# GNN layer with BatchNorm and LayerNorm on one core: other places for the gathered edge groups, bf16 parts read in place, and a row phase in eight pieces

## What is computed

```
msg   = x[src] + edge_feat                       # 53125 x 128
neigh = segment_sum(msg, dst, 3125)
rst   = (1 + eps) * x + neigh
h     = rst @ W1 + b1                            # 3125 x 256
h     = relu((h - mean(h,0)) * rsqrt(var(h,0) + 1e-5) * gamma + beta)
out   = layernorm(x + h @ W2 + b2)               # rows of 128
```

## Time and profile before

| | us |
|---|---|
| median of 3 runs | 280.74 (280.03 to 281.6) |
| the profiled execution | 281.48 |
| its span, first to last instruction | 279.7 |
| PE busy | 244.9 |
| weight loads | 200.6 |
| VectorE busy | 208.4 |
| ScalarE busy | 131.7 |
| GpSimd busy | 181.2 |

### The profile page before, as it was taken

The page is one execution under the profiler, slowest core; times in us unless marked ns, Lnnn a source line. Parts: engine busy times, 40 slices in busy tenths (PEclk is TensorE's granted clock), DMA queues, the critical chain, the costliest instruction groups (busy, mean ns, idle before and its releaser), DMA issues.

```text
span 279.7 us, 7102 instructions
## 1 busy us (share of the span) xinstructions
PE 244.9 (88%) x2211; PEld 200.6 (72%) x2211; DVE 208.4 (75%) x916; ACT 131.7 (47%) x236; POOL 181.2 (65%) x117
## 2 busy tenths in 40 slices
PE   1567989999998889988899999999999859999970
PEld 1456768899987677766788888777878648844870
DVE  3888997788998778778489887876867861178990
ACT  0327864455555535545255544444443302086494
POOL 2078888888888888888888888888888920000000
PEclk9999999999999999999599999999999968999995
DMA  5955766687888777788488888776665200000033
GB/s 165 285 172 108 147 145 137 156 191 197 189 195 185 178 164 171 181 179 183 96 172 192 174 195 171 167 179 145 150 126 105 53 2 0 2 0 1 2 114 116
DMA packets 49535, 38.39 MB, mean 137 GB/s; under 512 B 5083, under 2 KB 48523, under 8 KB 49497
## 3 DMA queue, kind: packets, MB, share of 16 engines
q1 hardware_dynamic: 32829, 30.62, 38.2%
q0 software_dynamic: 14976, 6.82, 20.4%
q10 hardware_dynamic: 1692, 0.48, 0.9%
HBM read 36.31 MB, written 1.60 MB: 136 GB/s over the span
## 4 chain that ended last, share of the span: by engine, by line
PE 46%; DMA 16%; issue 14%; POOL 9%; DVE 7%; ACT 4%; SPq 2%; DVEq 0%; ACTq 0%; POOLq 0%
PE ps L641 18%; PE ps L649 12%; DMA egat<-in_x_dram,srci 9%; POOL egat L402 9%; DMA egat<-in_edge_attr_dram 7%; PE ps L679 5%; PE ps L673 4%; PE ps L595 4%; ACT big L527 3%; PE ps L665 2%; SPq L321 1%; DVE big L1033 1%; DVE big L1035 1%; PE ps L670 1%; DVE hit_l L904 1%
## 5 line engine op out<-in xcount | busy, mean ns | idle before, releaser
L402 POOL DMA_INDIRECT egat<-in_x_dram,srci x104 | 172.2, 1656 | 44.0 <-issue 29.2
L488 ACT ACTIVATE big<-ps 128x500 f32 x156 | 95.1, 610 | 119.8 <-PE ps L679 91.6
L641 PE MATMUL ps<-big,xp 128*128 128x114 f16 (+8 forms) x675 | 116.9, 280 | 0.2 <-issue 0.2
L649 PEld LDWEIGHTS ps<-hit_c,ebuf 128*128 128x128 f32 x624 | 101.8, 194 | 16.6 <-DVE aggT L983 6.1
L649 PE MATMUL ps<-hit_c,ebuf 128*128 128x20 f32 x624 | 95.1, 230 | 9.1 <-DVE aggT L983 5.0
L641 PEld LDWEIGHTS ps<-big,xp 128*128 128x128 bf16 x675 | 63.0, 110 | 14.6 <-issue 1.1
L983 DVE TENSOR_TENSOR aggT<-aggT,ps 128x20 f32 x208 | 35.8, 172 | 49.8 <-PE ps L649 39.7
L910 DVE TENSOR_TENSOR hit_k<-iota_k,key 128x400 f16<-128x400 f16 x156 | 56.1, 359 | 0.0
L904 DVE TENSOR_TENSOR hit_l<-iota_k,lo 128x256 f16<-128x256 f16 x156 | 52.1, 334 | 1.7 <-issue 1.6
L679 PE MATMUL ps<-hit_k,hit_l 128*128 128x400 f16 x156 | 52.3, 335 | 0.0
L908 DVE TENSOR_TENSOR hit_k<-iota_k,key 128x300 f16<-128x300 f16 x156 | 48.2, 309 | 0.0
(11 more groups left out here) (101 smaller groups left out, 165.5 us busy)
## 6 DMA issues: line engine op xcount, KB each, us to landing
ebuf<-in_edge_attr_dram SPq DMA_DIRECT2D x78, 256.0 KB
egat<-in_edge_attr_dram SPq DMA_DIRECT2D x51, 128.0 KB
egat<-in_x_dram,srci POOLq DMA_INDIRECT x104
out_dram<-big SPq DMA_DIRECT2D x6, 256.0 KB
w_sb<-in_L_gnn_W_dram ACTq DMA_DIRECT2D x2, 128.0 KB, 6.8
rows<-in_dst_dram SPq DMA_DIRECT2D x1, 192.0 KB
rows<-in_src_dram ACTq DMA_DIRECT2D x1, 192.0 KB
egat<-in_edge_attr_dram SPq DMA_DIRECT2D x1, 66.0 KB
```

The lines of the kernel that those rows point to most:

```text
L402: return nc.gpsimd.indirect_dma_start(to, None, x[:, :], bass.IndirectOffsetOnAxis(ap=ix, axis=0), compute_op=op)
L488: nc.scalar.activation(cnt[:, :, bass.ds(lows[m % LOADS], WIN)], ps[:, m % BANKS_C, 0:KEYS].rearrange("p (t n) -> p t n", n=WIN), ACT.Copy ...
L641: last = nc.tensor.matmul(ps[:, ACC + f % 2, 0:SIZES[f]], xp[:, t, n, :], cnt[:, t, STARTS[f]:STARTS[f] + SIZES[f]], start=(u == 0), stop= ...
L649: last = nc.tensor.matmul(ps[:, SUMS + w % BANKS_S, 0:WIN], rows_v[:, j * D:(j + 1) * D], hits_v, start=(j == 0), stop=(j == ROWS - 1))
```

## The change

1. **Places of the gathered windows.** `arrange` replaces `in_window`. It walks through the windows with a running cost `now` in PE cycles and takes the next gathered group as soon as now has reached GATHER_FIRST + n * GATHER. 207 stays the last gathered window.
2. **bf16 parts in place.** `xp` and ScalarE's 14 copies go. The matmuls read the upper halves of xN and of a full-size `xr` where they lie, every second 16-bit value; only the third part has a tile of its own (`x3`).
3. **GpSimd's addition of b2** now waits for the last block's product (`block_multiplied`, 9), since xN is read until then.
4. **Ring of `hit_k`, `hit_l`:** 8 places instead of 6.
5. **Row phase:** eight pieces of 4, 4, 4, 4, 4, 2, 2 and 1 row tiles on eight banks. ReLU of half 1 of blocks 5 and 6 goes to ScalarE (one step instead of two). Piece 6 is normalised by VectorE from PSUM. VectorE takes the statistics of a piece ahead of the shifts of the piece before.

```diff
-RING_K = 6
+RING_K = 8
+ROUNDS = 12
+SUM = 670
+COUNT = 770
+KEPT = 810
+HITS = 2400
+TURN = 1680
+GAP = 14
+GATHER = 9360
+GATHER_FIRST = 27000
+ACT_FROM = 5
...
-    def in_window(w):
-        return (w + 1) * NG // G > w * NG // G
+    def arrange():
+        order = [(w + 1) * NG // G > w * NG // G for w in range(G)]
+        for _ in range(ROUNDS):
+            ready = spans([w for w in range(G) if not order[w]])
+            now, m, n, order = 0, 0, 0, []
+            for w in range(G):
+                gathered = n < NG - 1 and w < G - 1 and (m == GC or now >= GATHER_FIRST + n * GATHER)
+                gathered = gathered or w == G - 1
+                f, u0, u1 = share(ready, w)
+                own = SUM if gathered else max(SUM + COUNT + KEPT * (m < KEEP), HITS)
+                now += own + (u1 - u0) * (SIZES[f] + GAP) + TURN * (X_RATE * w < NT)
+                order.append(gathered)
+                m, n = m + (not gathered), n + gathered
...
+    ROW_PIECES = [(t, t + 4) for t in range(0, NT - 5, 4)] + [(NT - 5, NT - 3), (NT - 3, NT - 1), (NT - 1, NT)]
...
         xN = sb("xN", [P, NT, D])
-        xp = sb("xp", [P, NT, PARTS, D], BF16)
+        xr = sb("xr", [P, NT, D])
+        x3_room = sb("x3_room", [P, NT * D // 2])
+        x3 = x3_room[:, :].bitcast(BF16).rearrange("p (t d) -> p t d", d=D)
...
                 pool.wait_ge(x_rest_made, NB)
-                pool.wait_ge(x_first_made, NB)
+                pool.wait_ge(block_multiplied, F)
...
+                if b >= ACT_FROM:
+                    hb = hT[:, 1, b * BANK:b * BANK + width(b)]
+                    nc.scalar.activation(hb, hb, ACT.Relu, scale=scl[:, 1:2], bias=sft[:, 1:2]).then_inc(relu_half0_made, 1)
...
+            deviation(0)
+            for a in range(1, 5):
+                deviation(a)
+                normalise(a - 1)
+            normalise(4)
+            deviation(5)
+            deviation(6)
+            normalise(5)
+            deviation(7)
+            normalise(7)
...
-                        last = nc.tensor.matmul(ps[:, ACC + f % 2, 0:SIZES[f]], xp[:, t, n, :],
+                        part_v = x3[:, t, :] if n == 2 else upper((xN, xr)[n][:, t:t + 1, :])[:, 0, :]
+                        last = nc.tensor.matmul(ps[:, ACC + f % 2, 0:SIZES[f]], part_v,
...
-            for b in range(NB):
+            for b in range(ACT_FROM):
                 r = rl[:, b % 2, 0:width(b)]
...
+            for a in range(len(ROW_PIECES)):
+                stats(a)
+                if a > 0:
+                    shifts(a - 1)
+                moments(a)
+            t0, t1 = ROW_PIECES[6]
+            dve.wait_ge(row_shifts_made, 7)
+            for t in range(t0, t1):
+                k = (t - t0) * D
+                nc.vector.tensor_scalar(oN[:, t, :], ps[:, 2, k:k + D], lrs[:, t:t + 1], lnb[:, t:t + 1],
+                                        ALU.mult, ALU.add).then_inc(late_rows_normalised, 1)
+            shifts(7)
```

More of the change, by code:

```diff
@@ L82, in gnn_layer, with spans, share @@
     KEYS = NT * WIN
-    def in_window(w):
-        return (w + 1) * NG // G > w * NG // G
-    C_AT = [w for w in range(G) if not in_window(w)]
-    G_AT = [w for w in range(G) if in_window(w)]
+    UNITS = NT * PARTS
+    def spans(c_at):
+        return [c_at[g - 1] + SETTLE for g in ENDS[:-1]] + [G]
+    def share(ready, w):
+        for f in range(F - 1):
+            if ready[f] <= w < ready[f + 1]:
+                n, i = ready[f + 1] - ready[f], w - ready[f]
+                return f, UNITS * i // n, UNITS * (i + 1) // n
+        return 0, 0, 0
+    def arrange():
[11 more added lines that the diff above has]
+                m, n = m + (not gathered), n + gathered
+            short = NG - sum(order)
+            at = [w for w in range(G) if not order[w]]
+            for w in at[len(at) - short:] if short > 0 else []:
+                order[w] = True
+        return order
+    IN_WINDOW = arrange()
+    C_AT = [w for w in range(G) if not IN_WINDOW[w]]
+    G_AT = [w for w in range(G) if IN_WINDOW[w]]
     C_OF = {w: m for m, w in enumerate(C_AT)}
     G_OF = {w: n for n, w in enumerate(G_AT)}
-    READY = [C_AT[g - 1] + SETTLE for g in ENDS[:-1]] + [G]
-    UNITS = NT * PARTS
+    READY = spans(C_AT)
     def units(w):
[L95 to L99, removed]
+        return share(READY, w)
+    ROW_PIECES = [(t, t + 4) for t in range(0, NT - 5, 4)] + [(NT - 5, NT - 3), (NT - 3, NT - 1), (NT - 1, NT)]
     EARLY = STARTS[-1] // BANK
@@ L1035, in _ @@
                 nc.vector.tensor_scalar(hb, r, 0.0, None, ALU.max).then_inc(relu_half1_made, 1)
[L1037 to L1054, removed]
-                                                   in1=lrs[0:r, t0:t1], op0=ALU.mult,
-                                                   op1=ALU.mult).then_inc(row_shifts_made, 1)
@@ new lines, in stats, with moments @@
+            def stats(a):
+                t0, t1 = ROW_PIECES[a]
+                r = rows_of(t1 - 1)
+                dve.wait_ge(rows_made, a + 1)
+                for t in range(t0, t1):
+                    k = (t - t0) * D
+                    nc.vector.bn_stats(lst[0:r, t, :], ps[0:r, (a + 4) % 8, k:k + D]).then_inc(row_stats_made, 1)
+            def moments(a):
+                t0, t1 = ROW_PIECES[a]
+                r = rows_of(t1 - 1)
+                for t in range(t0, t1):
+                    dve.wait_ge(row_stats_made, t + 1)
+                    nc.vector.bn_aggr(lag[0:r, t, :], lst[0:r, t, :]).then_inc(row_moments_made, 1)
```

92 lines of the change are left out of this document (42 added, 50 removed).

## The result

The changed kernel takes 292.09 us (median of 4 runs, 291.27 to 292.7), beside 280.38 us (279.57 to 281.6) for the kernel before on the same chip: a ratio of 1.041, 95% interval 1.036 to 1.046, so 11.7 us slower. Its profiled execution took 291.68 us, its span is 289.9.

A forecast was written before the change was run, and what follows sets the result against it. GpSimd's gather stream, one group per 3.8 us, was taken to bound PE where it waits. Loop +12.0, addition 0, parts 0, tail +0.3 made +12.3 on 281.48: 293.8 profiled, 293 us as median, range 285 to 300.

The forecast's parts named there:

- window 184 starts: PE, window of group 50: gathered rows there at 216.0 us, plus 1.1 for the clock, so start at 217.1 us.
- work behind it, to the hidden layer: PE's windows from 184 on and last block's products, at full clock without the stall: 38.2 us.
- end of the loop against before: Loop over the windows: ends at 255.3 us against 243.27, +12.0 us.
- addition of b2 beside the hidden layer: GpSimd's addition after the loop: covered or not held up, bounds 0 and 7.6 us, taken as 0.
- parts in place, copies, ring of eight: Front copies and ring gain 0; spread weight loads cost 0 to 10 us, taken as 0.
- row phase: Tail after the hidden layer: earlier statistics against more hand-overs, bounds -1.0 and +1.3 us, taken as +0.3.
- The stream: GpSimd's gathers: 33 groups after group 17 at 3.81 us each, rows on PE 2.7 us after the last gather ends.
- The term of 1.1 us: PE's lateness from half clock shortly before window 184, taken between 0 and 2.4 us.
- This sign of the forecast: PE's waits for gathered rows in the new profile: far above 7.9 us, some 20 to 25 us in 35 or more.
- The rival that it holds VectorE up after the loop: GpSimd's addition of b2 delays the last block's addition and hidden layer by 7.6 us: 300.6 us, chance 0.05.
- The rival of slow loads: PE's spread weight loads are slow, adding up to 10 us: some 298 to 303 us, chance 0.08.
- two readings of the Trainium skill: PE's weight loads: strided columns load fast, cost stays 0; or 32-bit reads leave half the bits unused, cost rises.

The follow-up runs named there:

- half_the_gathers: The changed kernel, same places, with GpSimd gathering only one of the two rows per partition, so the sums are incomplete: 261.68 us (one run).
- new_places_only: The kernel before with only the new places of the gathered windows: 300.47 us, ratio 1.075.
- places_by_pe_cost: The changed kernel with planner constants HITS 1440 instead of 2400, GATHER 9120 and GATHER_FIRST 20000: 264.90 us, ratio 0.946.

## Why the prediction was right

It held, in sign, in size (293 against 292.09) and in its mechanism: window 184 had to wait for group 50's rows, and 39 us of counted work stood behind it. That the two numbers lie 0.9 us apart is partly luck. Of the steps below one is 2.3 us too late, one 0.8 us too short and one 0.6 us too long, and they partly cancel; and between the profiled executions the loss is 291.68 - 281.48 = 10.2 us where +12.3 was forecast, while the medians lie 11.7 us apart. Step by step:

| step | predicted | measured |
|---|---|---|
| window 184 starts | 217.1 us | 214.8 |
| work behind it, to the hidden layer | 38.2 us | 39.0 |
| end of the loop against before | +12.0 us | +10.5 |
| addition of b2 beside the hidden layer | 0 | 0 |
| parts in place, copies, ring of eight | 0 | 0 |
| row phase | +0.3 us | -0.3 |
| profiled execution | 293.8 us | 291.7 |

**The stream.** The forecast started from group 17's second gather at 86.07 and went on at 3.81 us a group. It started at 87.10, and the next 33 groups took (211.39 - 87.10) / 33 = 3.77 us each. The rows were on PE 1.9 us after the gather's end, not 2.7. Together 1.03 - 1.4 - 0.8 = -1.2 us.

**The clock at window 184.** The term of 1.1 us didn't come: the last stretch at half clock before window 184 (197.6 to 201.0) was made good by then. That is the rest of the 2.3 us between 217.1 and 214.8.

**The waits.** This sign of the forecast failed: predicted were 20 to 25 us in 35 or more waits, it was 14.0 us in 17, and at window 184 itself PE stood only 0.26 us. The slack was there, but in another form. Between 60 and 215 us PE ran 10.2 us at half clock from 81.5, 10.2 from 108.9, 3.4 from 149.8 and 3.4 from 197.6: 27.2 us, in which by an estimate from the clock 13.6 us of full-speed work were not done. 14.0 + 13.6 = 27.6 us lost against the stream, of the size of the 30 us that half_the_gathers gives back. In the two long ones, below, PE is busy for 10.20 of 10.20 us: at half clock it arrives late and doesn't stand. For the end it is the same, since the stream sets it, and the wait of 0.25 us at 211.09 and of 0.26 at 214.82 says that PE had caught up.

```profile
81.50:91.70 10.20, 10.20 (x63) 8.85 (x63) 5.25 (x24) 3.17 (x5) 8.68 (x6) 0.50 0.57 114
108.90:119.10 10.20, 10.20 (x57) 8.80 (x56) 5.58 (x26) 3.20 (x5) 8.42 (x6) 0.50 0.57 114
```

(The changed kernel, by stage, columns as in the earlier trace rows.)

**What is left behind window 184.** 0.8 us too little. Twelve of the 13 windows of 466 columns took the 1.18 us that were taken from the earlier trace rows, the last, where the block changes, 1.43; windows 198 to 205, each from its start to the next one's, took 1.75 to 1.88 us and the last 2.24, together 14.8 against 14.4. half_the_gathers, in which window 184 starts 30 us earlier, has the same 38.9 us: it is PE's work and not a wait.

**The addition of b2.** The rival that it holds VectorE up after the loop is refuted: VectorE's statistics beside it, timeline of the changed kernel, take what they took before, 0.69 us each; and the last block's addition (253.99 us, 0.27 long) starts before GpSimd's does at 254.35.

```profile
258.21 0.69 DVE L1057 BATCH_NORM_STATS2 big<-big 128x6 f32<-128x512 f32 x1 [0.17 <-ACT big L537]
```

The same addition beside a hit instruction with two SBUF inputs made that one last 8.07 us in new_places_only, where the short one in the same kernel took 0.28. The two cases agree with the rule that the prediction took from the Trainium skill (SBUF — State Buffer, Who interferes with whom): beside a GpSimd instruction that reads SBUF, a VectorE instruction with two SBUF inputs contends, and one with a single SBUF input, outside the modes that use two ports, doesn't.

**Weight loads in place.** The rival of slow loads is refuted too. In the changed kernel a load from xN took 110 ns on the mean and a packed one from `x3` (x_room in the rows) 114, where they took 110 before, each over all widths of product; the last block's 75 products start 0.048 us apart in both kernels. Of the two readings of the Trainium skill (TensorE: Matmul & The Clock Gate, Weight-path perf modes) this supports the one by which strided columns load as fast as packed ones; that 32 bits are read at a time shows no cost here.

**The row phase.** Right to 0.6 us, but not by the steps given: VectorE did stop for ScalarE, at piece 5, for 2.06 us, which no step named, and two hand-overs to ScalarE near the end left it idle for 0.59 and 0.57 us, not 0.3. What made up for this was not looked for.

**Two readings that were off.** Group 10 is at window 44, not 40 (that is group 9). Groups 0 to 11 stand up to four windows later than before, 12 to 14 where they stood, and only from group 15 on each is asked for earlier. And the order on PE that stands for windows 183 and 184 of the kernel before has the waits of windows 191 and 192: group 47 is the one in slot 5, group 45 is in slot 3. The sum uses neither.

**Why the places are too early.** The prediction took the order as given and didn't ask why the planner had chosen it. What `HITS` is charged for is the answer that the record supports. The runs with 1440 in its place take 264 to 266 us, some 26 to 28 below the changed kernel's 292.09, with either start. The smaller `GATHER` in them isn't what helps: worked out from the code, `arrange` with GATHER 9120 alone puts group 50 at window 182, earlier still, and with HITS 1440 alone at 206, as in those runs. It also comes to 206 if 2400 is kept and compared with a counted window's whole cost, its units included. None of these three orders was run by itself.

## What to carry to other kernels

When work is put in an order by a table of costs, compare each cost with the duration in the trace before judging the order, and ask whether costs of two engines that work side by side are added: here one term, 1.0 us for what takes PE 0.6, made a list of waits out of a good idea. Where one engine's stream supplies another in strict order, find the last item that is supplied and count what stands behind it; while the stream is the slower one, that remainder, added to the stream's end, is the time, whatever happens before. A change that as a whole loses can hold a part that gains, here the later addition with 5.2 us, so try each part alone.

## What the runs showed of the hardware that was not expected

- Half clock came in stretches of up to 13.7 us. After a standstill of 1.71 us PE ran at 0.50 for 10.2 us, after one of 1.95 us for another 10.2; in places_by_pe_cost 13.7 us began during a standstill of 1.33 us. Before, 1.85 us had been followed by 6.8, and a standstill of 1.54 us (up to 24.20) by none: the clock was 1.00 from there to 33 us. What sets the fall and its length stays open; no run was made for it.
- Gathered rows can be on PE 1.9 us after the gather's end on GpSimd, against 2.4 to 4.0 read before.
- The addition of b2 takes 7.54 us on GpSimd beside VectorE's two-input instruction and 6.97 beside the one-input ones: GpSimd's lasts 0.57 us longer, while VectorE's is drawn out from 0.28 to 8.07 us.
